# Plain fp32 matmuls for the shared down product, q/k/v and the projection, and no keep-warm matmuls in the attention steps

## The reference, cut to what matters

```python
x = x + 0.5 * ffn(layernorm(x))        # 8192 tokens of 128 values
x = x + attn(layernorm(x))             # 32 rows of 256 tokens
x = x + 0.5 * ffn(layernorm(x))        # the same weights again

def ffn(x):
    top_v, top_i = top_k(x @ gate_w, 2)            # 8 experts
    expert_out = ...                               # 2 experts a token, inner width 352, softmax weights
    shared = silu(x @ Sg) * (x @ Su) @ Sd          # inner width 176
    return expert_out + shared

def attn(x):                                       # linear attention, 16 heads of 8
    q, k, v = split(x @ W_attn + b_attn)
    q, k = elu(q) + 1, elu(k) + 1
    num = running sum over the tokens of (k outer v), times q
    den = running sum of k, times q, + 1e-6
    return (num / den) @ W_proj + b_proj
```

## Time and profile before

| | |
|---|---|
| time, median of 3 runs | 1369.38 us (1367.43 to 1383.91) |
| span of the profiled execution | 1240.9 us, 31979 instructions |
| the profiled execution's whole time | not given; only its span is |
| mean granted clock of PE | 0.930 of full |
| DMA | 86.62 MB, mean 70 GB/s |

### The profile page before, as it was taken

One profiled execution on the slowest core, in us unless ns is written; L12 is line 12 of the kernel. 1 busy time (PEld: TensorE's weight loads), 2 busy tenths in 40 slices (PEclk: granted clock), 3 DMA queues, 4 the chain that ended last, 5 costly groups with the idle time before them and its releaser, 6 DMA issues. The chain is left out here.

```text
span 1240.9 us, 31979 instructions
## 1 busy us (share of the span) xinstructions
PE 989.7 (80%) x8996; PEld 742.7 (60%) x8997; DVE 896.8 (72%) x2369; ACT 669.6 (54%) x1466; POOL 843.8 (68%) x872
## 2 busy tenths in 40 slices
PE   2657665999999927788888888888864999999940
PEld 1434344899989924455555555555543888899930
DVE  6778784676676745788888888888854666666748
ACT  4556642555555523466665656666331555555545
POOL 4677773777777845467787787778642677777750
PEclk9898996999999968999999999999966999999985
DMA  9411122222222221001111111100003222222229
GB/s 279 108 51 47 52 76 66 78 79 76 78 77 78 68 59 33 17 33 37 34 34 51 34 38 41 41 17 18 23 27 87 74 74 77 78 75 78 73 95 332
DMA packets 68607, 86.62 MB, mean 70 GB/s; under 512 B 13004, under 2 KB 56209, under 8 KB 68558
## 3 DMA queue, kind: packets, MB, share of 16 engines
q1 hardware_dynamic: 51278, 52.15, 14.5%
q0 software_dynamic: 17280, 33.87, 8.3%
HBM read 44.74 MB, written 43.04 MB: 71 GB/s over the span
## 5 line engine op out<-in xcount | busy, mean ns | idle before, releaser
L496 POOL DMA_INDIRECT expert_results<-ey,eidx x284 | 293.3, 1033 | 70.9 <-issue 69.6
L485 POOL DMA_INDIRECT routed_rows<-row,idx x256 | 255.2, 997 | 73.6 <-issue 70.2
L1142 DVE SCALAR_TENSOR_TENSOR ehT<-eh,ehT 128x768 f16<-128x768 f32 x142 | 136.1, 958 | 150.1 <-ACT ehT L688 150.1
L683 ACT ACTIVATE esil<-PSUM 128x768 f32<-128x768 f32 x142 | 115.1, 810 | 230.2 <-PE PSUM L826 224.6
L824 PE MATMUL PSUM<-eT,WGU 128*128 128x256 f16 x852 | 234.3, 275 | 1.4
L825 PE MATMUL PSUM<-eT,WGU 128*128 128x256 f16 x852 | 233.9, 275 | 0.0
L826 PE MATMUL PSUM<-eT,WGU 128*128 128x256 f16 x852 | 233.8, 274 | 0.0
L510 POOL TENSOR_TENSOR space<-qk,val 128x1152 f32<-128x1152 f32 x64 | 138.2, 2171 | 69.5 <-DVE shift L1192 48.7
L824 PE MATMUL PSUM<-WD,ehT 128*128 x852 | 161.0, 220 | 8.3 <-DVE ehT L1142 5.0
L825 PE MATMUL PSUM<-WD,ehT 128*128 x852 | 159.3, 220 | 0.0
L826 PE MATMUL PSUM<-WD,ehT 128*128 x852 | 158.8, 219 | 0.0
(11 more groups left out here) (197 smaller groups left out, 2300.0 us busy)
## 6 DMA issues: line engine op xcount, KB each, us to landing
xe<-routed_rows SPq DMA_DIRECT2D x142, 130.0 KB, 2.1
space<-expert_results SPq DMA_DIRECT2D x32, 512.0 KB, 3.9
expert_results<-ey,eidx POOLq DMA_INDIRECT x284
X<-in_L_attn_x_dram SPq DMA_DIRECT2D x16, 256.0 KB, 4.6
routed_rows<-row,idx POOLq DMA_INDIRECT x256, 2.3
out_dram<-X SPq DMA_DIRECT2D x16, 256.0 KB, 4.3
routed_rows<-pad_rows SPq DMA_DIRECT2D x24, 130.0 KB
space<-in_L_ffn_Wg_dram SPq DMA_DIRECT2D x1, 1408.0 KB, 9.1
```

The costliest lines, as they stand in the source:

```text
L485: pool.indirect_dma_start(routed, bass.IndirectOffsetOnAxis(ap=idx[u][:, k, j:j + 1], axis=0), row[u][:, j, :], None).then_inc(s_scattered ...
L496: pool.indirect_dma_start(result, bass.IndirectOffsetOnAxis(ap=eidx[u][:, h:h + 1], axis=0), ey[u][:, h, :], None, bounds_check=K * T - 1, ...
L683: act.activation(esil[u][:, :], PSUM[:, 1536 * u:1536 * u + 768], ACT.Silu, scale=2.0 ** -(SX + SWT)).then_inc(s_block_silu, 1)
L1142: return dve.scalar_tensor_tensor(out=dst, in0=src, scalar=float(2 ** scale), in1=high, op0=ALU.mult, op1=ALU.subtract)
```

## The change

The three products keep their operands in fp32 and are one plain matmul each; the splitting of hidden values, attention rows and y goes, and so do the weights' splits. `hidden` is two SBUF tiles that are used in turn, in place of one area of PSUM. The nine `keep_warm` matmuls of an attention step go; the six of the first stage stay. The scales `SH` of the shared expert and `SY` go. What is left of the diff (declarations and scale factors are cut):

```diff
-        SDW = sb("SDW", [P, 2, SC * D], F16)
-        AW = sb("AW", [P, 2, 3 * D], F16)
-        PW = sb("PW", [P, 2, D], F16)
+        SDW = sb("SDW", [SW, SC * D])
+        AW = sb("AW", [P, 3 * D])
+        PW = sb("PW", [P, D])
...
-        shT = sb("shT", [SW, 2, SC, GT], F16)
+        hidden = [sb(f"hidden{u}", [SW, SC, GT]) for u in range(2)]
...
@@ sync: the same loads, into other tiles
-            for w, n in ((gate_w, E), (sg, FS), (su, FS), (w_attn, 3 * D), (w_proj, D)):
+            for w, n in ((gate_w, E), (sg, FS), (su, FS)):
...
+            sp.dma_start(AW[:, :], w_attn).then_inc(s_small_weights, 16)
+            sp.dma_start(PW[:, :], w_proj).then_inc(s_small_weights, 16)
...
@@ gpsimd, attention step
-                        if ready:
-                            low(m + 2, xa[:, 1, :, :], 1, xa[:, 0, :, :], s_attn_high, s_attn_low)
...
+                    pool.drain()
                     streams_of(pool, step)
@@ scalar
-            def shared_high(n):
-                act.wait_ge(s_shared_hidden, n * UNITS + UNITS)
-
-                wait(act, s_shared_out, n)
-                act.activation(shT[:, 0, :, :], HIDDEN[ffn[0]], ACT.Copy).then_inc(s_shared_high, 1)
...
-                normalize(xn[:, 1, :, :], 1, m)
-                act.activation(xa[:, 0, :, :], xn[:, 1, :, :], ACT.Copy).then_inc(s_attn_high, 1)
+                normalize(xn[:, 1, :, :], 1, m).then_inc(s_attn_rows, 1)
...
-                act.activation(xaT[:, :, :], PT[:, :].rearrange("p (a t) -> p a t", a=2), ACT.Copy).then_inc(s_xaT, 1)
+                act.activation(xaT[:, :], PT32[:, :], ACT.Copy).then_inc(s_xaT, 1)
...
-            def y_high(m):
+            def y_evacuate(m):
                 act.wait_ge(s_y_turned, m + 1)
-                act.activation(yaT[:, 0, :], PT32[:, :], ACT.Copy, scale=float(2 ** SY)).then_inc(s_y_high, 1)
+                act.activation(yaT[:, :], PT32[:, :], ACT.Copy).then_inc(s_yaT, 1)
@@ tensor
             def ups(n, u):
-                wait(pe, s_shared_low, n)
+                wait(pe, s_shared_hidden, n * UNITS)
...
-            def down(n, m=None):
-                pe.wait_ge(s_shared_low, n + 1)
+            def down(n, u, m=None):
+                pe.wait_ge(s_shared_hidden, n * UNITS + UNITS)
...
-                        h = slice(c * D, (c + 1) * D)
-                        mm = product(POS[ffn[0]][:, j * D:(j + 1) * D], [shT[:, 0, c, t], shT[:, 1, c, t]],
-                                     [SDW[0:SW, 0, h], SDW[0:SW, 1, h]], start=(c == 0), stop=(c == SC - 1))
+                        mm = pe.matmul(POS[ffn[0]][:, j * D:(j + 1) * D], hidden[u][:, c, t], SDW[:, c * D:(c + 1) * D],
+                                       start=(c == 0), stop=(c == SC - 1))
...
             def attention_transposes(m):
-                pe.wait_ge(s_attn_low, m + 1)
+                pe.wait_ge(s_attn_rows, m + 1)
...
-                transpose_group(lambda part, j: xa[:, part, j, :], s_attn_turned)
+                for j in range(NJ):
+                    mm = pe.transpose(PT32[:, j * P:(j + 1) * P], xn[:, 1, j, :], ident32[:, :])
+                mm.then_inc(s_attn_turned, 1)
...
-                product(PG[a][:, 0:3 * D], [xaT[:, 0, t], xaT[:, 1, t]], [AW[:, 0, :], AW[:, 1, :]], start=False
-                        ).then_inc(s_qkv_products, 1)
+                pe.matmul(PG[a][:, 0:3 * D], xaT[:, t], AW[:, :], start=False, stop=True).then_inc(s_qkv_products, 1)
...
-                    mm = product(POS[ffn[0]][:, j * D:(j + 1) * D], [yaT[:, 0, t], yaT[:, 1, t]], [PW[:, 0, :], PW[:, 1, :]],
-                                 start=False, stop=(j == NJ - 1))
+                    mm = pe.matmul(POS[1][:, j * D:(j + 1) * D], yaT[:, t], PW[:, :], start=False, stop=(j == NJ - 1))
...
                     running_sums(m + 1, 0, 1)
-                    keep_warm(9)
@@ vector
-            def shared(n, c):
+            def shared(n, u, c):
...
+                if c == 0:
+                    wait(dve, s_shared_out, n - 1)
...
-            def shared_low(n):
-                dve.wait_ge(s_shared_high, n + 1)
-                low(shT[:, 1, :, :], HIDDEN[ffn[0]], shT[:, 0, :, :], 0).then_inc(s_shared_low, 1)
...
-            def y_low(m):
-                dve.wait_ge(s_y_high, m + 1)
-                low(yaT[:, 1, :], PT32[:, :], yaT[:, 0, :], SY).then_inc(s_yaT, 1)
```

More of the change, by code:

```diff
@@ L576, in normalize @@
                 for j in range(NJ):
-                    act.activation(dst[:, j, :], xs[:, j, :], ACT.Identity, scale=rstd[:, slot, j:j + 1],
-                                   bias=shift[:, slot, j:j + 1])
-                act.drain()
+                    last = act.activation(dst[:, j, :], xs[:, j, :], ACT.Identity, scale=rstd[:, slot, j:j + 1],
+                                          bias=shift[:, slot, j:j + 1])
+                return last
             def norm_first(g, v, known):
@@ L585, in norm_first @@
                 normalize(PXN, v, g)
+                act.drain()
             def high_first(g, v):
@@ L805, in _ @@
             evacuate(0, 0)
-            part(SDW[0:SW, 0, :], small_w[0:SW, o + 4 * D:o + 4 * D + SC * D]).then_inc(s_weights_high, 1)
             groups(act, first_ffn)
@@ L1127, in _ @@
             groups(pe, first_ffn)
-            down(NG - 1)
+            down(NG - 1, 1)
             phase_end(pe, 1)
@@ L1503, in streams @@
                     attend(m + 1, 1, 0)
-                if settle:
-                    if end:
-                        ends()
-                        tables()
-                    shared_low(n - 1)
+                if settle and end:
+                    ends()
+                    tables()
                 if ready:
```

93 lines of the change are left out of this document (31 added, 62 removed).

## The result

After the change the kernel takes 1384.59 us (median of 20 runs, 1370.65 to 1400.49), before it 1375.96 (20 runs, 1361.11 to 1384.42): ratio 1.0076, interval 1.0048 to 1.0103. The change was to win 20.7 us and loses 8.6. The forecast was 1349 (said as 1350); the time lies 35.9 us above it, of which 6.6 are the base (median 1375.96 over 20 runs, where the prediction had 1369.38 over three) and 29.3 the saving that did not come (20.7 + 8.6).

A forecast was written before the change was run, and what follows sets the result against it. Attention was taken as bound by a back-and-forth chain through DVE, POOL, PE and ACT, not one engine. Attention -15.7 and first stage -5.0 gave -20.7 us, from 1369.4 to 1349 (said as 1350), range 1320 to 1374.

The forecast's parts named there:

- the base of the sum: Whole kernel: profiled span 1240.9 us plus a constant 128.5 gives the median 1369.4, from which the saving is taken.
- the four rivals: Waits close 1322 us, chance 0.20; off the path 1363, 0.08; loads exposed 1369, 0.13; clock 1399, 0.07.
- Price of an fp32 matmul: PE, 128 columns: 0.11 us an instruction taken, between bounds 0.107 and 0.20, if weight loads stay hidden.
- The third rival: PE's fp32 weight loads exposed at 128 columns, 0.20 us an instruction; attention step +0.7 us, 1369 us; chance 0.13.
- First stage: First feed-forward stage: -3.8 us for POOL's wait, -1.2 for the group before, together -5.0.
- POOL's wait of the earlier trace: First stage: POOL's 4.39 us wait at 56.22 for DVE's row positions goes, to under 1.
- PE's wait of 5.5 us for shT: First stage: PE sat 5.51 us until 48.31 as `ups` waited for shared_low; called the cause of POOL's wait.
- Steps -2 to 0: Steps around the start of attention: step -2 saves 1.1 us, step -1 2.0, step 0 0.6.
- The last steps: End of the attention stage: step 14 saves 0.6 us, the two last ones about 1 each, an estimate.
- The full step: Attention: 26.84 less 0.12 and 0.60 gives 26.12 us, -0.72 a step, -9.4 over thirteen.
- turns into a wait for PE and pays nothing: Attention step on DVE: shared_low's removed 1.13 us becomes a wait for PE at attend, with no gain.
- The clock rival: Attention without keep-warm: PE's clock falls to 1.2 GHz, running sums take twice 3.87 us; up to 1399 us; chance 0.07.

The follow-up runs named there:

- attn_only: Kernel before with the attention part alone (fp32 q/k/v and projection, scale constant left old), keep-warm and shared expert as before: 13.0 us faster than before.
- sets 6 and 9: Semaphore raised late, behind the next step's running sums: projection's in before 1.0763, in after 1.0677 (6); positions' in after 0.9834 (9).
- set 7: keep_warm(24) in place of keep_warm(6) in the first stage, slower condition: in before 1404.14 us (1.0093), in after 1434.42 us (1.0241).

## Why the prediction was wrong

**The step that failed** is the base of the sum: "the median of the runs, 1369.4, lies 128.5 above that span, which I carry over as a constant". That time is not outside the span and not constant. It is TensorE results that come late in all stages, and with the change it grew from 135.0 us (1375.96 in the slower condition, 1240.93 in the faster) to 164.7 (1384.59 and 1219.88). A span 9% under the median should have said that the profile shows a kernel without something that its timed runs have, and that every saving read from it holds for that condition alone. None of the four rivals had it.

**The saving itself was right**, in the condition of the profile: -20.7 forecast, -21.1 and -22.8 measured (19.5 and 20.4 by the ratios). That it fits so closely is in part luck: by stages, first, between, attention and rest, the forecast was about -5.0, -3.7, -10.0 and -2 and the profiles give -3.5, -3.6, -13.5 and -0.9. By its terms:
- Price of an fp32 matmul: 0.112 us from start to start, forecast 0.11. The third rival (loads exposed, 0.20) is out: the recorded load of 192 ns hides, since the pace is 0.112. The prediction says that the trace of before shows no such pair behind 107 ns; one stood near, the fp32 transposes of y, with loads recorded at 140 ns, whose last three follow one another at 0.109 us:

```profile
660.63 0.66 PE L957 MATMUL PSUM<-ident,space 128*128 128x128 f32 x4
```

  Where the clock is at its lower level, in the first stage, sixteen down matmuls take 3.76 us, 0.22 from start to start, which the sum left out. The rule of the Trainium skill, "TensorE: Matmul & The Clock Gate", on the FP32 load told the direction of the recorded load, and not the pace. The estimate of 107 ns for the load is not the 190 to 192 ns that are recorded.
- First stage: forecast -5.0, measured -3.5. POOL's wait of the earlier trace rows did not go: it is 5.92 us at 57.73 where under 1 was expected. PE's wait of 5.5 us for shT did go, and in its place PE waits 7.29 us for ACT's xT ahead of the logits; so `ups` was not what held POOL. In after, in the faster condition:

```profile
51.35 0.38 PE L831 MATMUL PSUM<-GW,xT 128*128 128x16 f16 x8 [7.29 <-ACT xT L596]
...
57.73 0.19 POOL L476 TENSOR_TENSOR ticket<-ones 128x1 f32<-128x1 f32 x1 [5.92 <-DVE idx L1199]
```

  What was won there is a little in some groups, 9.5 to 8.7 us between two choices in the middle of a loop.
- Steps -2 to 0: forecast -3.7, measured -3.6 (between). The last steps: about -1 after the last choice.
- The full step: forecast 26.84 to 26.12. Steps mostly alternate in before (26.9 and 27.8, mean 27.3), and I had read a short one; after, they are all 26.1 to 26.6, mean 26.3. So -1.0 a step: 0.5 from the attention part (mean 26.8 in attn_only), 0.5 from keep-warm (after against after with keep-warm: 6.5 us over 13 steps), as forecast, and nothing from the shared expert's.
- shared_low "turns into a wait for PE and pays nothing": the shared part alone leaves attention at 399.5 against 398.4, and DVE waits 1.02 us where about 1 was forecast. The sums start right behind the outer product (712.29 + 2.17, then 0.05 us), the choice doesn't wait for the logits, and the clock stays at 1.00. In after, the faster condition:

```profile
712.29 4.29 POOL L499 TENSOR_TENSOR space<-qk,val 128x1152 f32<-128x1152 f32 x2 [2.18 <-DVE shift L1165]
...
714.51 2.20 PE L922 MATMUL PSUM<-space,upto 128*128 128x320 f32 x6 [0.66 <-POOL space L499]
...
723.74 1.36 DVE L1337 TENSOR_TENSOR prod<-PSUM,qk 128x1152 f32<-128x1152 f32 x1 [1.02 <-PE PSUM L924]
```

- The clock rival did not come. In the profile after the clock is 0.97 in the attention stretch; between 606 and 1000 us it is at its lower level (1.2 GHz) six times, each time in one of the seven long steps told below, after PE had waited 2.7 to 3.1 us for ACT's ssil.

**Where the 29 us went.** In the slower condition a late stretch of mostly 4 to 5 us comes in nearly every full step of either kernel. In before it falls on the positions in all but one step, and their reader comes 10 us later; in the new kernel it reaches the projection, whose readers (ACT's row words and residual, then DVE, then POOL) set the step. Seven groups of the profile after have the projection 4.2 us late or more, and the seven steps in which these stand last 29.5 to 31.0 us, the other full ones 26.2 to 26.7; a projection late by 1.5 costs nothing. The seven hold 29.0 us above 26.4 each, nearly all of attention's +31.9. In before attention has +7.0, of which some 4.5 is the one step with a late projection. The difference is 24.9 of the 29.7 us (21.1 + 8.6) to be explained; an estimate, good to some 3 us, since before's figure is from a kernel that differs in the first stage and from another set, and its attention stage has 398.4 to 401.5 in the faster condition. That the place decides the price is shown by sets 6 and 9, and by before's one long step in set 7. The remaining 5 us are not assigned.

**What stays open.** What makes the results late, and why the stretch opens before the projection's end in the new kernel. It is not tied to the part of the code that changed: against the same kernel's profile in the faster condition, the profile after has 40 us more in "between" and 48 in "rest", which are mostly the two expert stages. It isn't the refill of instructions either, as far as the trace shows it: the profile after and the same kernel's profile at 1217 us have the same 23 and 23 packets on the instruction queues, and in the former none between 283 and 512 us, where most of the first expert stage lies. The Trainium skill, "Runtime: NRT & Kernel Launch", section on instruction fetch mechanics, says that a taken branch to a target outside the window has to fetch by DMA before execution goes on; the late stretches aren't that, since TensorE goes on taking instructions in them. No run in the slower condition has one part of the change alone.

## What to carry to other kernels

Hold the span of a profile against the timed runs first. Here they belong within 2 us of each other; a span 128.5 us below the median was of another condition, and the difference answered to the change by more than the change's own terms. Then ask for each result of the engine that can come late how soon its reader stands there. A signal whose reader comes 10 us later took a delay of 5 us for nothing; one placed just ahead of a chain's entry took 1.5 us for nothing, and paid 4 us and more nearly in full.

Removing fp16 splitting paid where the helper engines' halves stand in the chain (y_low and the copies of the attention part, 0.5 us a step) and not where they turned into a wait (shared_low). The matmuls themselves cost a third more: two of fp32 at 0.112 us against three of fp16 at 0.056, 0.22 against 0.17 us for 128 columns.

## What was unexpected of the hardware

- The same kernel takes 1241 or 1369 to 1395 us by the condition, with recorded durations unchanged (the experts' L803 takes 274 ns in both) and much of the added time in waits that no instruction of the core is seen to end. TensorE's semaphores rise up to 4.5 to 6 us after the start of a last matmul that needs 0.2 to 0.45 otherwise, while up to fifteen more matmuls start.
- Nine keep-warm matmuls in a step hold nothing in the new kernel: its clock in attention is 1.00 with them and without them. In the old one it is 1.00 with them and 0.98 without, at the same time. In the first stage twelve raise the clock from 0.82 to 0.85 and cost 9 us, none lower it to 0.78, which costs nothing.
- The fp32 weight load of 128 columns is recorded at 190 to 192 ns, and yet such matmuls follow one another at 112 ns.
